# Four graph layers on one core: one gathered column in four chunks fetched row by row by SyncE, scale and maximum of edges 2 moved beside the pieces, and node 1's products taken in halves

## The reference, cut to what matters

```python
src_h = h[src]                                         # a row of 64 for every edge
se = concatenate([src_h, eh], axis=-1)
msg = leaky_relu(se @ W_msg, 0.01)
q = concatenate([qrh, qeh], axis=-1) @ W_q / sqrt(d)
k = se @ W_k
att = sum(q * k, axis=-1)
e = exp(att - segment_max(att, dst)[dst])
agg = segment_sum(e[..., None] * msg, dst) / segment_sum(e, dst)
x = layernorm(x + layernorm(leaky_relu(agg @ W_out) + h))
```

## Time and profile before

| | us |
|---|---|
| median of 3 runs | 9137.8 |
| lowest and highest run | 9130.26 and 9137.97 |
| the profiled execution | 9133.93 |
| its span, first to last instruction | 9132.2 |
| POOL busy | 6676.1 (73%) |
| VectorE busy | 5454.6 (60%) |

### The profile page before, as it was taken

The page is one execution under the profiler, slowest core; times in us unless marked ns, Lnnn a source line. Parts: engine busy times, 40 slices in busy tenths (PEclk is TensorE's granted clock), DMA queues, the critical chain, the costliest instruction groups (busy, mean ns, idle before and its releaser), DMA issues. The chain is left out here.

```text
span 9132.2 us, 36460 instructions
## 1 busy us (share of the span) xinstructions
PE 1872.5 (21%) x4249; PEld 957.9 (10%) x4249; DVE 5454.6 (60%) x6299; ACT 2476.6 (27%) x2302; POOL 6676.1 (73%) x6997
## 2 busy tenths in 40 slices
PE   3000000000200000000054444444434222222224
PEld 1000000000200000000032222222213101010104
DVE  5365656565657777777727777777766333333335
ACT  0122222232523232323231111111114333333333
POOL 6777777776777777777647777777765777777776
PEclk6555555555555555555576666676667656565656
DMA  8233333333123333333225555555542333333332
GB/s 354 82 108 109 108 109 108 111 106 106 31 91 106 107 108 105 111 102 113 86 79 183 179 175 186 178 175 186 178 138 71 115 121 115 121 115 123 113 123 82
DMA packets 384127, 1146.63 MB, mean 126 GB/s; under 512 B 163424, under 2 KB 194682, under 8 KB 362128
## 3 DMA queue, kind: packets, MB, share of 16 engines
q1 hardware_dynamic: 127984, 676.77, 19.7%
q0 software_dynamic: 249696, 445.02, 17.7%
q10 hardware_dynamic: 6336, 23.79, 0.7%
HBM read 736.78 MB, written 408.32 MB: 125 GB/s over the span
## 5 line engine op out<-in xcount | busy, mean ns | idle before, releaser
L783 POOL DMA_INDIRECT pair<-pair_table,edge_ix x1512 | 1480.5, 979 | 460.6 <-issue 460.6
L783 POOL DMA_INDIRECT g<-x_table,edge_ix x1512 | 1427.9, 944 | 460.8 <-issue 460.8
L783 POOL DMA_INDIRECT hidden<-hidden_table,edge_ix x1512 | 1426.7, 944 | 460.8 <-issue 460.8
L783 POOL DMA_INDIRECT qv<-qv_table,edge_ix x1484 | 1400.2, 944 | 452.2 <-issue 452.2
L921 ACT ACTIVATE edge_sums<-edge_val 128x1904 f32<-128x1904 f32 (+3 forms) x220 | 1112.4, 5056 | 459.8 <-DVEq L1535 459.8
L1340 PE MATMUL edge_pair_ps<-w_e,edge_eh_t 128*128 128x384 f32 x1568 | 916.4, 749 | 1101.4 <-DVEq L1393 1086.3
L864 ACT ACTIVATE edge_bank<-edge_weight_arg 128x112 f32<-128x112 f32 (+3 forms) x169 | 38.6, 228 | 3215.0 <-DVE edge_decay_arg L855 3215.0
L911 DVE TENSOR_TENSOR_SCAN edge_val<-edge_bank,edge_val 128x464 f32<-128x464 f32 (+1 forms) x715 | 687.6, 1032 | 358.0 <-ACT edge_val L1497 353.9
L1489 PE MATMUL edge_e_ps<-w_nodes,edge_ea_t 128*128 128x512 f32 x784 | 476.4, 773 | 1465.3 <-DVEq L1529 1456.6
L1528 DVE TENSOR_TENSOR hidden<-hidden,edge_e_ps 128x3584 f32<-128x3584 f32 x55 | 213.8, 3888 | 842.5 <-DMA hidden<-hidden_table,edge_ix 791.9
L1124 DVE TENSOR_TENSOR edge_product<-edge_k_ps,qv 128x896 f32<-128x896 f32 x112 | 185.7, 1658 | 690.7 <-DMA qv<-qv_table,edge_ix 683.4
(11 more groups left out here) (430 smaller groups left out, 5730.9 us busy)
## 6 DMA issues: line engine op xcount, KB each, us to landing
sums<-edge_sums SPq DMA_DIRECT2D x56, 1848.0 KB, 7.1
edge_q_in<-in_edge_attr_q SPq DMA_DIRECT2D x56, 1792.0 KB, 9.6
sums<-edge_sums SPq DMA_DIRECT2D x55, 1792.0 KB, 6.3
sums<-edge_sums SPq DMA_DIRECT2D x56, 1008.0 KB, 4.0
sums<-edge_sums SPq DMA_DIRECT2D x55, 924.0 KB, 4.1
edge_k<-k_edges SPq DMA_DIRECT2D x56, 896.0 KB, 4.6
edge_bond<-in_edge_attr SPq DMA_DIRECT2D x56, 896.0 KB, 8.3
edge_eh_t<-in_edge_attr_t SPq DMA_DIRECT2D x56, 896.0 KB, 4.7
```

The lines of the kernel that those rows point to most:

```text
L783: e.indirect_dma_start(self.gather_into(u, j), None, self.gather_from, bass.IndirectOffsetOnAxis(ap=now[:, j:j + 1], axis=0))\
```

## The change

There are three parts.

Edges 2: one addition now covers values and points of a piece, both in PSUM (L1463); behind the product come a scale by 0.01 from PSUM into `msg` (L1466) and a maximum of that and the PSUM values (L1468). The slot is given back after the maximum. The instruction on the whole `msg` is gone, as are the two of the cut chunk.

Node 1: `project` and `take_x` work on two halves of a group, with lags 10 and 11 on TensorE, 11 and 12 on ScalarE, and a semaphore for each half.

All edge phases: in every second round of the loop, POOL leaves out the last column of the second chunk (`with_aside`: 12 rounds in edges 0, 13 in each of the others). SyncE fetches it. In the round before, after the attributes of b = 0 and of b = 1, it takes rows 0 to 43 and 44 to 87; in the round itself, after the attributes of b = 0, rows 88 to 127. For up to 24 rows (`BATCH`) it loads the table's address and the numbers into registers from a new input, `src_aside`, which holds the skipped columns one after another, and issues a transfer of one row for each into the tile `aside`. Then it waits for all 128 rows and a free buffer, and one transfer places the tile as column 27. Consumers wait for `last_in` (the last column where POOL gathers it) and `placed`.

```diff
@@ sync
         def turn(i, beside=lambda b: None):
             for b in (0, 1):
                 for c in range(self.parts):
-                    self.wait_part(e, i, b, c)
+                    self.wait_part(e, i, b, c, placed=False)
                 load_index(b, bass.ds(i * (2 * J) + (2 + b) * J, J))
                 hold(e, self.attr_free[b], at(i, 1, 1), self.passed)
                 load(b, i * 2 + (2 + b))
+                beside(b)
                 hold(e, self.ready[b], at(i, 1, 1), self.passed)
                 store(b, rows_of(i, b, J))
 
+        def fetch(k, rows):
+
+            for first in range(rows.start, rows.stop, BATCH):
+                now = slice(first, min(first + BATCH, rows.stop))
+                _, numbers = p.nc.values_load_multi_w_load_instructions(
+                    p.ins["src_aside"][bass.ds(k + (self.steady + 1) // 2, 1), now],
+                    engines=[mybir.EngineType.SP], min_val=0, max_val=p.n_rows - 1,
+                    skip_runtime_bounds_check_because="src holds node numbers below n_nodes")
+                for r, number in zip(range(now.start, now.stop), numbers):
+                    e.dma_start(self.aside[r:r + 1, :], self.gather_from[bass.ds(number, 1), :])\
+                        .then_inc(self.aside_in, 16)
+
+        def place(i, k):
+
+            hold(e, self.aside_in, at(k, 16 * P, 16 * P), self.passed)
+            hold(e, self.rows_free[1], at(i, 1, 1), self.passed)
+            u = self.buffer(i, 1)[0]
+            e.dma_start(self.gather_into(u, J - 1), self.aside[:, :]).then_inc(self.placed, 16)
+
+        with e.Fori(0, (self.rounds - 1 - self.steady) // 2) as k:
+            one = k * 2 + self.steady
+
+            def beside_one(b):
+                if b == 0:
+                    hold(e, self.placed, at(k, 16, 1), self.passed)
+                fetch(k, ASIDE[b])
+
+            def beside_two(b):
+                if b == 0:
+                    fetch(k, ASIDE[2])
+                    place(one + 1, k)
+
+            turn(one, beside_one)
+            turn(one + 1, beside_two)
...
@@ gpsimd
-                    if J * n + j < done:
+                    if J * n + j < done or (b and j == J - 1 and i in self.with_aside):
                         continue
...
@@ edge_phase_2, weigh
-                e.tensor_tensor(points, two(g[b][:, cols, FD:]), points, ALU.add)
-                e.tensor_tensor(two(msg[:, cols, :]), two(g[b][:, cols, 0:FD]), values, ALU.add)
+                light = two(msg[:, cols, :])
+                e.tensor_tensor(made_now, two(g[b][:, cols, :]), made_now, ALU.add)
                 e.drain()
                 e.tensor_tensor(two(product[:, 0:slot, :]), two(q_in[b][:, cols, :]), points, ALU.mult)
+                e.tensor_scalar(light, values, 0.01, None, ALU.mult)
+                e.drain()
+                e.tensor_tensor(light, values, light, ALU.max)
                 e.drain().then_inc(used, 1)
...
-                e.scalar_tensor_tensor(msg[:, :, :], msg[:, :, :], 0.01, msg[:, :, :], ALU.mult, ALU.max)
-                e.drain()
...
@@ node_phase_1
-            def project(g):
+            def project(g, half):
+                now = halves_of(g)[half]
...
-            in_turn(groups, (1, turn_back), (8, turn_x), (10, project), per=4)
+            in_turn(groups, (1, turn_back), (8, turn_x), (10, lambda g: project(g, 0)), (11, lambda g: project(g, 1)), per=4)
...
-                    (11, take_x), per=4)
+                    (11, lambda g: take_x(g, 0)),
+                    (12, lambda g: take_x(g, 1)), per=4)
```

More of the change, by code:

```diff
@@ L682, in __init__ @@
         self.passed = self.sem("passed")
+        self.steady = self.alone + 1
+        self.aside = self.sb("aside", [P, p.gather_width[layer]])
+        self.aside_in, self.placed = self.sem("aside_in"), self.sem("placed")
+        self.last_in = self.sem("last_in")
         self.bank = self.ps("bank", [P, 512])
@@ L784, in gpsimd, with with_aside, wait_last @@
                                          bass.IndirectOffsetOnAxis(ap=now[:, j:j + 1], axis=0))\
-                        .then_inc(self.gathered[u][j * self.parts // J], 16)
+                        .then_inc(self.last_in if b and j == J - 1 else self.gathered[u][j * self.parts // J], 16)
+    @property
+    def with_aside(self):
+        return range(self.steady + 1, self.rounds - 1, 2)
+    def wait_last(self, e, i, placed):
+        if isinstance(i, int) and i <= self.steady:
+            e.wait_ge(self.last_in, 16 * (i + 1))
+            return
+        alone = ((i + (2 + self.steady)) >> 1) * 16
+        if not placed:
+            hold(e, self.last_in, alone, self.passed)
+        else:
+            e.wait_ge(self.last_in, alone)
+            e.wait_ge(self.placed, at((i - (self.steady - 1)) >> 1, 16, 1))
     def buffer(self, i, b):
@@ L793, in buffer, with wait_part @@
         return 1 - b, (i, 1, b)
-    def wait_part(self, e, i, b, c):
+    def wait_part(self, e, i, b, c, placed=True):
         u, (times, per, more) = self.buffer(i, b)
         columns = 16 * J // self.parts
-        e.wait_ge(self.gathered[u][c], at(times, per * columns, more * columns))
+        if c < self.parts - 1:
+            e.wait_ge(self.gathered[u][c], at(times, per * columns, more * columns))
+            return
+        if not self.begun:
+            e.wait_ge(self.gathered[u][c], at(i, columns - 16 * b, columns - 16 * b))
+        elif isinstance(i, int) and i < 2:
+            e.wait_ge(self.gathered[u][c], (columns, columns - 16, columns, 2 * columns - 16)[2 * i + b])
+        else:
+            more = columns if b else -16
+            if placed:
+                e.wait_ge(self.gathered[u][c], at(i, columns - 16 * b, more))
+            else:
+                hold(e, self.gathered[u][c - 1], at(i, columns, columns * b), self.passed)
+                hold(e, self.gathered[u][c], at(i, columns - 16 * b, more), self.passed)
+        if b:
+            self.wait_last(e, i, placed)
     def wait_gathered(self, e, i, b):
@@ L1996, in _ @@
             for g in range(groups):
-                e.wait_ge(x_taken, g + 1)
+                for half in (0, 1):
+                    after(e, x_taken[half], sum(1 for k in range(g + 1) if halves_of(k)[half]))
                 e.dma_start(table[:, ph.now(g), :], pair_out[g % outs][:, 0:ph.sizes[g], :])\
@@ L2047, in turn_x @@
                 last.then_inc(x_turned, 1)
-            def project(g):
+            def project(g, half):
+                now = halves_of(g)[half]
+                if not now:
+                    return
                 e.wait_ge(x_moved, g + 1)
-                after(e, x_taken, g)
-                for k in range(firsts[g]):
+                after(e, x_taken[half], sum(1 for k in range(g) if halves_of(k)[half]))
+                for k in now:
                     last = e.matmul(pair_banks[:, k, :], x_t[g % 2][:, k, :], p.w2_x, start=True, stop=True)
```

46 lines of the change are left out of this document (27 added, 19 removed).

## The result

The changed kernel takes 9083.5 us (median of 5 runs, 9082.06 to 9087.3) where the kernel before takes 9133.7 in the same comparison; the ratio is 0.9945, with a 95% interval of 0.993 to 0.9959. It is 50 us faster. The forecast was 124 us; the time lies inside the range, 12 us from the 9095 that rival A was given.

A forecast was written before the change was run, and what follows sets the result against it. POOL's gathers were taken to bound the kernel, an edge phase being as long as its gathers. From 9133.9 us, -50 + 3 - 13 - 63.7 = -124 gave 9010, with a range of 8990 to 9120.

The forecast's parts named there:

- rival A: Edges 2: SyncE comes late, since a pair of loads costs 4.7 us and the loop 145; about 9095 us; chance 0.26.
- the tail: End of edges 2: nothing covers VectorE's added work there, +3 us.
- the one beside L1390: Edges 2: the gather beside L1390, a sum reading PSUM, keeps its 0.95 us; taken as sign that new operations hold none.
- The bill on VectorE: Edges 2: scale and maximum at 0.414 us each, net +3.7 us a chunk, 1.5 us a chunk left.
- A turn: Node 1: one round of the ScalarE and TensorE ring, 6.34 us, to get 1.1 us shorter, near 5.25; -13 in all.
- the price of the loads: SyncE: a pair (address, numbers) taken at two index-transfer trips, 3.4 us; six pairs in two rounds, 20 us.
- the loop of edges 2: Column placed, VectorE to the end of the next chunk's pieces, SyncE's three turns, landing: 137 us against POOL's 138.6.
- a late column: Edges 2: VectorE's wait for the placed column, taken as 0, and 13 us for each us above.
- Its far end: Rival A's span, 9010 to 9165 us; the end is pairs of 5.6 us, or rows at 0.64 us.
- B: SyncE loop, all four phases: SyncE cannot keep the rate, slower than before, some 11320 us at 1.2 a row; chance 0.14.
- C: Edges 2: gathers stay held or VectorE becomes the bound, so 50 us don't come, 9060 us; chance 0.08.
- D: Fetched columns: the 51 are not saved, only if another engine sets a chunk's end, which is A or C; no own chance.

The follow-up runs named there:

- the run with rows first: The changed kernel, but in edges 2 SyncE issues a turn's rows ahead of its wait for free attributes and of the attribute transfers: 9013.1 us (0.9867).

## Why the prediction came out as it did

**Part 1 was right.** Forecast -50 for the gathers and +3 for the tail, found -48.4 in the gathers' busy time (1480.5 to 1432.1) and +3.7 behind the last gather (14.1 to 17.8 us), -45.3 in edges 2 (2031.4 to 1986.1). The new operations do not hold gathers, as the one beside L1390 said. The bill on VectorE was right too: a scale of 0.418 and a maximum of 0.425 where 0.414 was taken, and 34.2 us a chunk, 0.8 us below POOL's 35.0 where the prediction left 1.5. On the rule of the Trainium skill ("SBUF — State Buffer", section "SBUF: two separate sides") this case says: operations with an input in PSUM left the gathers alone, as it has it; how much two SBUF inputs hold POOL depends here on how long one instruction lasts (0.42 us: hardly, 2.02 us: 0.9 us of delay).

**Part 2 was right.** A turn of 5.25 us was forecast, 5.24 came; node 1 lost 15.9 us, a little past the -13 and the -15 of its range's end.

**Part 3 was right in its rate and in three phases.** 38 columns at 1.249 us are 47.5; edges 0, 1 and 3 lost 13.2, 15.5 and 15.7 us, 44.4, and the two experiments with and without the fetch there differ by 50 (47 between their profiled executions). No gather of these phases waits.

**The step that failed is the price of the loads, in the loop of edges 2.** The prediction had the loop, all its members, and what it costs to miss it (13 us for each us above 138.6). It put it at 137 us with 1.6 us to spare, and so took 0 for a late column. It is 144.5; the 5.9 us above POOL's pace, 12 to 13 times, are 71 to 77 us, and edges 2 ended 75 above its forecast. Term by term:

| member of the loop, us | predicted | measured |
|---|---|---|
| VectorE, to free attributes | 38 | 41.8, with the column's landing |
| 128 rows | 70 (0.55 each) | 52.7 (0.412 each) |
| six pairs of loads | 20 (3.4 each) | 40 (38.2 and gaps) |
| SyncE's other transfers | 5 | 10, with the rows' landing |
| landings | 4.5 | in the rows above |
| sum | 137 | 144.5 |

The rows were taken 17 us too dear and the loads 20 us too cheap; the rest is some 4 us short. The loads' term, 20 us forecast and 40 found, is the one whose price came from no like row: it took two trips of the index transfer, and did not ask what SyncE had put into the queues just before. Six quiet pairs would take some 21 us (an estimate from the quiet ones of the run with rows first), as forecast; half of the pairs are not quiet. The error in the rows hid most of that in the loads. Had only the rows been priced at their 0.41 us, the forecast would have had 19 us to spare in the loop.

So rival A is what happened, in its place and with its mechanism, a loop that the loads make too long. That its numbers came out near (a loop of 145 us and 9095 us forecast, 144.5 and 9083.5 measured) is luck: it had 70 us of rows and 28 of loads, where 53 and 40 were found. With its pairs of 4.7 us and rows of 0.41 the loop would have been some 128 us and the column in time. It had a chance of 0.26 against 0.52. With a margin of 1.6 us out of 138.6 beside two prices whose bounds lay apart by factors of nearly three and of four hundred, the two should have stood at least even. Its far end was also added up wrongly: rows of 0.64 us give a loop of 148.6 us and 9139, not 9165.

The estimate from the Trainium skill ("Runtime: NRT & Kernel Launch", section "Instruction fetch mechanics", about 200 ns a register) gave 4.8 us for 24 numbers and 9130 us. (It took every load at 24 numbers; they have 24 and 20 twice, then 24 and 16.) The quiet loads here are 0.11 us a number, about half of it; behind the attribute transfers of edges 2 a load of 24 takes 4.5 to 6.5 us on average. The pointer to rival A was right, the cause was another: not the number of registers, but the transfers just ahead.

**The other rivals.** B did not come near: a row costs 0.41 us where it was to decide at 0.85, and a pair 6.4 on average where it was to decide at 9.7. C: no gather is held, and VectorE keeps 0.8 us a chunk. D: in the three other phases every column left out is a column saved.

**What stays open.** Node 2 takes 2.8 to 5.4 us more than before in all kernels traced here, also in the one that changes only edges 2's last operation; no run separates its cause. The stretch ahead of the first gather is 4 to 7 us shorter in every kernel with part 2, unexplained. Nor does any run show why a held gather was held longer in the kernel without part 1 than in the kernel before.

## What to carry to other kernels

An engine with free time is no cover for work that it does in a fixed place of a loop: follow the loop through every engine that waits in it, and compare its length with the pace of the bound before counting the savings. Two savings can be bought from the same slack: here part 1 shortened the pace of the bound by some 4 us and lengthened by as much the loop that part 3 needed. Work that needs nothing from the others goes ahead of the waits in an in-order queue, not behind them: moving a fetch some lines up turned 50 us of gain into 121.

## What the runs showed of the hardware that I had not expected

A register load on SyncE takes 1.1 us for an address and some 0.11 us for each number (0.9 us for 8, 1.7 to 1.8 for 16, 2.5 to 2.8 for 24) where no large transfer goes just ahead of it. In edges 2, right behind the queue's own 896 and 1792 KB, an address took 2.5 to 5.2 us and 24 numbers 3.9 to 7.2. A transfer of one row with its register work takes 0.412 us, 0.228 of it the issue, where issues in the earlier trace rows took 0.33. The loop of SyncE has become 494 records of the trace long where it was 33, and from its branch back to the next record 4.8 us pass (5123.37 to 5128.19; 4.7 to 6.4 in all phases) where it was 0.1 to 0.3; here VectorE's work covers it.
